# K's bias added by VectorE, ScalarE's bias rows, and value rows spread by identity columns

## The reference

```python
mod = (_silu(c) @ wmod).reshape(16, 6, 1, -1)          # sa, ca, ga, sb, cb, gb
h = _layernorm(x) * (1 + ca) + sa
# attention on h
Q = elu(h @ Wq + bq) + 1;  K = elu(h @ Wk + bk) + 1;  V = h @ Wv + bv
KV = einsum('nshd,nshm->nhmd', K, V);  Ksum = K.sum(axis=1)
Z = 1 / (einsum('nlhd,nhd->nlh', Q, Ksum) + 1e-6)
y = einsum('nlhd,nhmd,nlh->nlhm', Q, KV, Z) @ Wo + bo
x1 = layer_norm(h + y) * g1 + beta1
z = layer_norm(x1 + relu(x1 @ W1 + b1) @ W2 + b2) * g2 + beta2
x = x + ga * z
h2 = _layernorm(x) * (1 + cb) + sb
# channel mix on h2, with h2 shifted by one token as x_prev
out = x + gb * sigmoid(xr @ W_r.T) * (square(relu(xk @ W_k.T)) @ W_v.T)
```

## Time and profile before

| | |
|---|---|
| median of three runs | 163.07 us (162.75 to 163.19) |
| the profiled execution | 162.81 us, span 160.7 us |
| busy: PE, PEld | 155.6 us (97%), 145.1 us (90%) |
| busy: DVE, ACT, POOL | 123.1, 127.3, 104.6 us |
| granted PE clock | 1.00 over the span |
| DMA | 9.94 MB, mean 62 GB/s |

### The profile page before, as it was taken

The page is one execution under the profiler, slowest core; times in us unless marked ns, Lnnn a source line. Parts: engine busy times, 40 slices in busy tenths (PEclk is TensorE's granted clock), DMA queues, the critical chain, the costliest instruction groups (busy, mean ns, idle before and its releaser), DMA issues.

```text
span 160.7 us, 4111 instructions
## 1 busy us (share of the span) xinstructions
PE 155.6 (97%) x1151; PEld 145.1 (90%) x1151; DVE 123.1 (77%) x572; ACT 127.3 (79%) x346; POOL 104.6 (65%) x243
## 2 busy tenths in 40 slices
PE   7899999999999999999999999999999999999992
PEld 6778998999999999999999999999999999888891
DVE  3766878597887969696978779796969777888842
ACT  4256777889797979898997979797989989656562
POOL 4337567576676767787676767676877755973631
PEclk9999999999999999999999999999999999999999
DMA  4926299920010101010100101010101001010112
GB/s 122 269 90 174 67 276 369 423 115 0 2 37 0 33 0 33 4 37 0 34 5 0 33 4 35 0 35 4 33 0 35 4 0 33 2 37 0 35 33 67
DMA packets 8974, 9.94 MB, mean 62 GB/s; under 512 B 724, under 2 KB 7416, under 8 KB 8952
## 3 DMA queue, kind: packets, MB, share of 16 engines
q1 hardware_dynamic: 8656, 9.60, 18.8%
q10 hardware_dynamic: 296, 0.08, 0.2%
HBM read 7.55 MB, written 2.13 MB: 60 GB/s over the span
## 4 chain that ended last, share of the span: by engine, by line
PE 93%; DMA 2%; DVE 2%; ACT 1%; issue 0%; SPq 0%; DVEq 0%
PE bank L1266 16%; PE bank L1156 16%; PE bank L1145 8%; PE bank L1238 5%; PE bank L1194 5%; PE bank L1150 5%; PE bank L1222 4%; PE bank L1182 4%; PE bank L1230 4%; PE bank L1378 4%; PE bank L1210 4%; PE bank L1206 4%; PE bank L1249 3%; DMA kqvo<-in_kqvo 2%; PE bank L1219 1%; PE bank L1398 1%
## 5 line engine op out<-in xcount | busy, mean ns | idle before, releaser
L1156 PE MATMUL bank<-w,hid 128*128 128x128 f32 x240 | 31.7, 275 | 0.0
L1266 PE MATMUL bank<-x1T,w 128*128 128x256 f32 x120 | 30.9, 381 | 0.0
L1156 PEld LDWEIGHTS bank<-w,hid 128*128 128x128 f32 x240 | 29.3, 192 | 0.0
L347 ACT ACTIVATE hid<-bank,b_cols 128x256 f32<-128x256 f32 x60 | 26.0, 511 | 1.1 <-PE bank L1266 1.1
L544 POOL TENSOR_TENSOR rstd_n<-vare_n,power 128x2 f32<-128x2 f32 x30 | 23.8, 792 | 2.4
L1266 PEld LDWEIGHTS bank<-x1T,w 128*128 128x128 f32 x120 | 21.5, 190 | 2.7 <-DVE z L803 0.2
L710 DVE TENSOR_SCALAR ny<-bank,mv_ny,rstd_ny 128x128 f32<-128x128 f32 x32 | 11.7, 406 | 9.0 <-POOL rstd_ny L544 9.0
L323 ACT ACTIVATE hT<-bank,modT 128x256 f32<-128x256 f32 x16 | 9.0, 565 | 11.3 <-PE bank L1145 11.3
L540 POOL TENSOR_TENSOR vare_n<-mv_n,eps 128x2 f32<-128x2 f32 x30 | 5.9, 195 | 17.2 <-DVE mv_n L704 17.1
L292 ACT ACTIVATE n<-x_all,shift_n,rstd_n 128x128 f32<-128x128 f32 x27 | 11.8, 485 | 2.5 <-POOL shift_n L552 2.5
L317 ACT ACTIVATE keepT<-bank,modT 128x255 f32<-128x255 f32 x26 | 13.1, 555 | 0.0
(11 more groups left out here) (187 smaller groups left out, 454.7 us busy)
## 6 DMA issues: line engine op xcount, KB each, us to landing
gm_rows<-mod_rows_dram SPq DMA_DIRECT2D x2, 960.0 KB, 9.5
out<-out_sb SPq DMA_DIRECT2D x15, 128.0 KB, 1.8
gm_rows<-mod_rows_dram SPq DMA_DIRECT2D x1, 768.0 KB, 6.7
w<-in_w SPq DMA_DIRECT2D x1, 512.0 KB, 5.6
x_all<-in_x SPq DMA_DIRECT2D x1, 512.0 KB, 5.6
bv_row<-bv_rows_dram SPq DMA_DIRECT2D x1, 512.0 KB, 7.1
bv_row<-bv_rows_dram SPq DMA_DIRECT2D x1, 384.0 KB, 4.4
gm_rows<-mod_rows_dram SPq DMA_DIRECT2D x1, 384.0 KB, 3.7
```

Of the source, the lines that this page charges most:

```text
L347: last = nc.scalar.activation(hid[:, f, :], bank[:, f % 2 * L:(f % 2 + 1) * L], ACT.Relu, bias=b1_cols[:, f:f + 1])
L1156: last = nc.tensor.matmul(banks[6][:, c * D:(c + 1) * D], hid[:, f, c * 128:(c + 1) * 128], w2[:, f, :], start=False, stop=(f == FF - 1 an ...
L1266: return nc.tensor.matmul(bank[:, f % 2 * L:(f % 2 + 1) * L], w1[:, f * 128:(f + 1) * 128], x1T[:, :], start=True, stop=True)
```

## The change

1. **K's bias.** For items 1 to 15 `k_product` no longer starts with the bias matmul. DVE adds the bias: `k_biased(s)` reads bank 4 and `bias_rows` and writes `kb` in SBUF. `k_exponent` and `k_elu` read `kb` from then on, and the bank is free for the next writer once `kb` is made. For item 0 the bias goes in through a f32 matmul of the identity with `bias_rows`.
2. **The bias rows.** `bias_rows` is made in the opening by PE (Wk's product with `bo`, minus `bk` through one row of -1) and one ACT operation; the bf16 split on DVE and its tiles go.
3. **The opening.** The first transposes take an `n1` made as `(x - mean) * rstd` by DVE (`normalise`), which needs no shift; the first `hT` gets a shift column of its own (`shift_first`). ACT makes both halves of the `n1` that the state product needs. Three warm-up matmuls go.
4. **Value rows.** `bv_product` is one matmul, early; DVE adds `bv` (`bv_rows`), and `direct_row(s)` is one matmul of an identity column, broadcast, with `bv_rows`.
5. **The step on DVE.** `centred` comes first, then `denominators`, `reciprocals`, `k_biased`, `attention`; the K half of the mix moves ahead of `k_elu`; the statistics of x are taken two items ahead, at the end of the step. POOL's `first_scale` moves behind `norm_scale("ny")`; `rstd` and `shift` of `n1` have two buffers.

```diff
+            act.wait_ge(bias_mm, 1)
+            act.wait_ge(const_pool, 1)
+            nc.scalar.activation(bias_rows[:, :], banks[6][:, D:2 * D], ACT.Identity, scale=-1.0,
+                                 bias=one_pair[:, 0:1]).then_inc(bias_rows_ok, 1)
...
             def k_exponent(s):
-                need(act, k_mm, s + 1)
-                nc.scalar.activation(exp_k[:, :, :], chunked(banks[4]), ACT.Exp, bias=neg1[:, :]).then_inc(expk_ok, 1)
+                if s == 0:
+                    act.wait_ge(k_mm, 1)
+                need(act, kb_ok, s)
+                source = kb[:, :, :] if s else chunked(banks[4])
+                nc.scalar.activation(exp_k[:, :, :], source, ACT.Exp, bias=neg1[:, :]).then_inc(expk_ok, 1)
...
-                h_turned(0)
+                act.wait_ge(hT_mm, 1)
+                nc.scalar.activation(hT[0][:, :], banks[0][:, 0:L], ACT.Identity, scale=mod_col(CA, 0),
+                                     bias=shift_first[:, :]).then_inc(hT_ok, 1)
+                n1_part(0, 1).then_inc(n1_ok, 1)
...
+                if live(t + 2):
+                    first_scale(sa + 2)
...
+            normalise("n1", n1[1], x_chunk(0), 1, n1_turn)
             dve.wait_ge(cols_mm, 1)
             nc.vector.tensor_scalar(modT[:, CA, :], banks[1][:, 0:S], 1.0, None, ALU.add).then_inc(cols_ok, 1)
+            nc.vector.tensor_tensor(shift_first[:, :], banks[1][:, 128:129], cols[:, BO:BO + 1], ALU.add).then_inc(cols_ok, 1)
...
             def k_elu(s):
                 need(dve, expk_ok, s + 1)
-                nc.vector.scalar_tensor_tensor(k_sb[:, :, :], exp_k[:, :, :], 1.0, chunked(banks[4]), ALU.min,
-                                               ALU.max).then_inc(k_ok, 1)
+                plain = kb[:, :, :] if s else chunked(banks[4])
+                nc.vector.scalar_tensor_tensor(k_sb[:, :, :], exp_k[:, :, :], 1.0, plain, ALU.min, ALU.max).then_inc(k_ok, 1)
+
+            def k_biased(s):
+                need(dve, k_mm, s + 1)
+                need(dve, bias_rows_ok, 1)
+                nc.vector.tensor_tensor(kb[:, :, :], chunked(banks[4]), bias_rows[:, :].unsqueeze(1).broadcast_to([128, NC, D]),
+                                        ALU.add).then_inc(kb_ok, 1)
...
                 x_stats(1)
                 x_mv(1)
+                dve.wait_ge(bv_loaded, 16)
+                dve.wait_ge(bv_mm, 1)
+                nc.vector.scalar_tensor_tensor(bv_rows[:, :], bv_bias[:, :], 1.0 / 128, banks[6][0:S, 2 * D:3 * D], ALU.mult,
+                                               ALU.add).then_inc(bv_ok, 1)
                 k_elu(0)
                 direct_weights(0)
-                q_elu(0)
+                dve.wait_ge(hT_mm, 1)
                 n1_chunk(1, 0)
                 n1_chunk(1, 1).then_inc(n1_ok, 1)
+                q_elu(0)
                 dve.wait_ge(const_pool, 9)
...
                 reciprocals(0)
+                k_biased(1)
                 attention(0)
+                direct_weights(1)
                 k_elu(1)
...
                 attention(1)
+                k_biased(2)
                 y_norm(0)
...
+                if live(t):
+                    centred(sp_)
+                    denominators(sb_)
+                    reciprocals(sb_)
+                    k_biased(sa)
+                    attention(sb_)
+                    if live(t - 4):
+                        mix_half(K_W, sc)
+                    k_elu(sa)
+                    middle(sp_)
+                    need(dve, x2_ok, sp_ + 1)
+                    norm_stats("n3", lambda c: x2_p[:, c, :])
+                    if live(t - 4):
+                        mix_half(R_W, sc)
+                    norm_mv("n3", sp_ + 1)
+                    y_stats(sb_)
+                    q_elu(sa)
+                    norm_mv("ny", sb_ + 1)
+                    if live(t + 2):
+                        x_stats(t + 2)
+                        x_mv(t + 2)
+                    masked_state(sa)
+                    shift_of_n3(sp_)
+                    y_norm(sb_)
+                    return
+
...
             def bv_product():
 
-                nc.tensor.matmul(banks[6][0:S, 2 * D:3 * D], modT[:, ROW, :], wv, start=True, stop=False)
-                nc.tensor.matmul(banks[6][0:S, 2 * D:3 * D], part128[:, 0:S], bv_pad[:, :], start=False, stop=True).then_inc(bv_mm, 1)
+                pe.wait_ge(cols_ok, 4)
+                pe.wait_ge(wvo_loaded, 16)
+                nc.tensor.matmul(banks[6][0:S, 2 * D:3 * D], modT[:, ROW, :], wv, start=True, stop=True).then_inc(bv_mm, 1)
 
             def direct_row(s):
 
-                pe.wait_ge(cols_ok, 3)
-                pe.wait_ge(wvo_loaded, 16)
-                pe.wait_ge(bv_loaded, 16)
-                dest = banks[2][:, s * D:(s + 1) * D]
-                nc.tensor.matmul(dest, modT[:, ROW, s:s + 1].broadcast_to([128, 128]), wv, start=True, stop=False)
-                nc.tensor.matmul(dest, part128[:, :], bv_pad[:, :], start=False, stop=True).then_inc(direct_mm, 1)
+                pe.wait_ge(bv_ok, 1)
+                nc.tensor.matmul(banks[2][:, s * D:(s + 1) * D], ident[0:S, s:s + 1].broadcast_to([S, 128]), bv_rows[:, :],
+                                 start=True, stop=True).then_inc(direct_mm, 1)
 
...
             def k_product(s):
 
+                if s == 0:
+                    pe.wait_ge(bias_rows_ok, 1)
+                    nc.tensor.matmul(chunked(banks[4]), ident[:, :], bias_rows[:, :].unsqueeze(1).broadcast_to([128, NC, D]),
+                                     start=True, stop=False)
+                    bv_product()
+                elif s == 1:
+                    pe.wait_ge(k_ok, 1)
                 need(pe, hT_ok, s + 1)
-                need(pe, k_ok, s)
+                need(pe, kb_ok, s - 1)
                 need(pe, tanh_ok, s - 4)
-                nc.tensor.matmul(chunked(banks[4]), ones3[:, :], bias_parts[:, :].unsqueeze(1).broadcast_to([128, NC, D]),
-                                 start=True, stop=False)
                 for c in range(NC):
                     last = nc.tensor.matmul(banks[4][:, c * D:(c + 1) * D], hT[s % 2][:, c * 128:(c + 1) * 128],
-                                            wk, start=False, stop=(c == NC - 1))
+                                            wk, start=(s > 0 and c == 0), stop=(c == NC - 1))
                 last.then_inc(k_mm, 1)
...
+                pe.wait_ge(n1_turn, 1)
+                transpose_in(banks[0], n1[1], hT_mm)
                 k_product(0)
                 q_product(0)
-                bv_product()
+                direct_row(0)
                 state_product(0)
+                value_of_state(0)
+                n1_transposes(1)
+                second_modulation((2, 5), 2)
+                attention_product(0)
+
+                k_product(1)
+                q_product(1)
                 pe.wait_ge(direct_ok, 1)
                 direct_row(1)
-                value_of_state(0)
-                second_modulation((2, 5), 2)
-                n1_transposes(1)
```

More of the change, by code:

```diff
@@ L290, in take_n1 @@
                 wait_x(act, s)
-                for c in chunks:
-                    last = nc.scalar.activation(n1[s % 2][:, c, :], x_all[:, NC * s + c, :], ACT.Identity,
-                                                scale=rstd["n1"][:, c:c + 1], bias=shift_n1[:, c:c + 1])
+                for c in range(NC):
+                    last = n1_part(s, c)
                 last.then_inc(n1_ok, 1)
-            take_n1(0, (0,))
+            act.wait_ge(bias_mm, 1)
+            act.wait_ge(const_pool, 1)
+            nc.scalar.activation(bias_rows[:, :], banks[6][:, D:2 * D], ACT.Identity, scale=-1.0,
+                                 bias=one_pair[:, 0:1]).then_inc(bias_rows_ok, 1)
+            act.wait_ge(x_in[0], 16)
+            act.wait_ge(shift_n1_ok, 1)
+            n1_part(0, 0)
             act.wait_ge(cols_ok, 2)
@@ L367, in first_steps @@
                 state_out(0)
-                act.wait_ge(bv_mm, 1)
-                nc.scalar.activation(bv_rows[:, :], banks[6][0:S, 2 * D:3 * D], ACT.Copy).then_inc(bv_ok, 1)
+                act.wait_ge(cols_ok, 5)
+                h_turned(1)
                 raw_columns(0)
-                h_turned(1)
                 k_exponent(1)
@@ L708, in normalise @@
                 need(dve, rstd_ok[name], count)
+                scale = rstd_n1[0] if name == "n1" else rstd[name]
                 for c in range(NC):
-                    last = nc.vector.tensor_scalar(dest[:, c, :], source(c), mv[name][:, c, 0:1], rstd[name][:, c:c + 1],
+                    last = nc.vector.tensor_scalar(dest[:, c, :], source(c), mv[name][:, c, 0:1], scale[:, c:c + 1],
                                                    ALU.subtract, ALU.mult)
@@ L977, in step @@
-                if live(t):
-                    q_elu(sa)
-                if not y_first:
-                    norm_mv("ny", sb_ + 1)
-                if t == S:
-                    y_norm(sb_)
-                    gated(sc)
```

(9 more changed lines are left out.)

161 lines of the change are left out of this document (59 added, 102 removed).

## The result

The changed kernel takes 163.58 us (median of 10 runs, 163.48 to 163.94), the kernel before in the same session 162.94 (10 runs, 162.37 to 163.26). The ratio is 1.0044, 95% interval 1.0031 to 1.0058: slower, by 0.6 to 0.7 us. The profiled execution took 163.68, with a span of 161.9 against 160.7.

A forecast was written before the change was run, and what follows sets the result against it. It took the ScalarE chain from the ny transposes to the attT copy as pacing, with PE also at its limit. 0.77 + 0.20 + 0.12 - 0.06 = +1.03 us gave 163.84 or 164.1, taken as 164.0; range 163.2 to 165.3.

The forecast's parts named there:

- Part 1: K's bias matmul leaving PE for 15 of 16 items: 0.107 us each, 1.6 on PE alone, taken as 0 for steps 3 to 15.
- The rival that PE alone paces: Every removed PE slot counts, 15 x 0.107 = 1.6 us, giving 161.4; chance 0.13.
- the one that the source is free: K's sum is in time and reading SBUF costs nothing: steps stay at 8.78, some 162.8; chance 0.22.
- Part 2: K's sum on DVE in front of exp_k: +0.07 us a step, 0 to 0.15; 0.77 for steps 5 to 15.
- The source: exp_k on ACT reading kb from SBUF instead of the bank: +0.05 us a step, bounds 0 and 0.10.
- the lateness: exp_k waiting for DVE's sum in a steady step: 0.02 us late, from on time to 0.06 late.
- The rival of a sum 0.2 late: DVE's sum clearly late, passing one to one into attT and the step: 166.3 us at 0.2 late; chance 0.13.
- The idle time of 0.1 to 0.2 in front of the output product: Expected sign in the changed profile: idle time on PE's loads in front of the output product, released by attT.
- Step 4 at +0.20: Step 4 costs more because step 3's y_norm still holds VectorE, so z's statistics start some 0.26 later: +0.20 us.
- Step 3 at +0.12: Without keeps on ACT, exp_k waits for the sum, starting about 26.90 instead of 26.35: +0.12 us, 0.05 to 0.2.
- Opening at -0.06: Opening up to the first hidden product: of 0.6 us gained, 0.06 remains; bounds -0.5 and +0.15.

The follow-up runs named there:

- e1: Kernel before without K's bias product for batch items 1 to 15 (bias left out for them): 0.9991 of the kernel before.
- e11: Changed kernel without DVE's K bias sum for items 3 to 15 (bias left out), exp_k and k_elu reading the bank: 162.57 us, 0.9980 of the kernel before.
- e2: Kernel before with the attT copy put ahead of the first hidden activation on ScalarE: 1.0011 of the kernel before.
- e4: Changed kernel with the attT copy put ahead of the first hidden activation on ScalarE: 162.09 us, 0.9953 of the kernel before.
- e6: Changed kernel with K's bias sum written back into the bank, exp_k and k_elu reading it there: 1.0054 of the kernel before.
- e3: Kernel before without K's bias product for items 1 to 15 and with attT copied ahead of the first hidden activation: 0.9992 of the kernel before.
- e7: Changed kernel with K's bias sum behind centred, ahead of denominators and reciprocals on VectorE, in every step: 1.0028 of the kernel before.
- e12: As e9, with value rows of items 0 and 1 spread by a product over 128 partitions instead of 16: 161.69 us, 0.9910 of the kernel before.
- e9: Changed kernel, attT copy ahead of the first hidden activation in steps 4 to 15, K's sum ahead of denominators in step 3 alone: 161.73 us, 0.9919 of before.

## Why the prediction was right, and where it wasn't

Forecast 164.0 with 0.55 for slower; measured 163.58. From the medians of before that is +0.93 forecast and +0.64 measured.

- **Part 1 at nothing.** Right, for the reason given: e1 and e11 show the nothing, e2 and e4 that attT's place held it there. The rival that PE alone paces fell, and so did the one that the source is free (e6). What the prediction didn't see is that the same product also covered hT, so that behind an early attT it is worth 0.03 a step on the kernel before (8.74 in e3 against 8.77 in e2) and 0.06 in the changed order (8.71 in e4), not 0.107.
- **Part 2 at 0.07 a step.** Measured 0.06 (8.84 against 8.78 before, and against 8.78 in e11). The source is 0.04 to 0.05, the lateness 0.04 instead of 0.02, less 0.03 that attT got shorter (0.39 instead of 0.42, for which no run gives a reason). All three were seen in rows. The rival of a sum 0.2 late fell. The idle time of 0.1 to 0.2 in front of the output product, which was to show it, isn't printed in steady steps.
- **Step 4 at +0.20.** Steps 4 and 5 together cost 0.17, in another split: 0.03 and 0.14. e7, with its steps of 8.85, has 8.83 and 8.85 there: with step 3 mended, step 5 is no longer special.
- **Step 3 at +0.12.** A mis-sized term: it cost 0.24. The sum ended at 27.27 and exp_k started at 27.31, where 26.90 was expected. Of this 0.26 is the opening; counted from hT, exp_k came after 2.09 where 1.94 was expected (26.90 - 24.96), and attT after 3.57 instead of 3.42. The error is in when DVE comes to the sum, behind z's statistics, centred, den and the reciprocal. Some 0.1 of it can be read off: z's statistics start 0.17 ahead of hT instead of 0.28 and no longer wait for PE, because x's statistics, moved to the end of the step before "at no cost", now stand in front of them. e7 shows the place of the sum: with the sum ahead of den the step is 7.68 against 7.65 before.
- **Opening at -0.06.** The largest miss, and wrong by its sign: +0.26 in this profile. The gain was smaller than forecast and was gone earlier: 0.70 instead of about 1.0 at the second K product, 0.13 instead of 0.6 at the third, 0.03 instead of 0.49 at the second attention on DVE. The loss behind it, item 2's sum and exp_k's wait for it, was sized right: from that attention to attT 1.63 us (17.54 to 19.17), where 1.59 was expected (17.08 to 18.67) and 1.02 was before. Of the 0.46 that is missing at the attention, about 0.16 is the pace of the first microseconds (below), and 0.11 the second value row over 16 partitions: its 0.28 had been priced at nothing, and 0.11 is what e12 still has of them there. The other 0.2 is open. In e9, with the same opening at a faster pace, step 3 starts 0.10 later than before, not 0.06 earlier.

The terms came to +1.03, and the spans differ by 1.2 in the profiles and 1.0 in the medians. That the sum fits is in part luck: the opening and step 3 cost 0.44 more than their terms, steps 4 to 15 0.20 less (0.77 instead of 0.97). And the forecast put the same 2.1 us around the span of both kernels, where the changed one has 1.75; without that it would have been nearer the measured 163.58, but no term of it foresaw this. The stated range is wider than its own reason: 0.01 and 0.13 a step alone give 163.3 to 164.7.

## What to carry to other kernels

Look at how far each weight load leads its matmul. In these traces the same load leads by 0.11 where its operand is early and by 0.05 or less where it is late; that wait shows in no idle time and hardly in busy shares, and the tile that the load waits for names the chain that paces. Take work from an engine only after asking what the removed instruction was covering; here it covered one wait (attT) outright and half of another (hT). Where two limits lie this close, neither edit alone gives anything: e1 nothing, e2 nothing, and one line moved behind another in the changed kernel, with its lighter TensorE, 1.5 us (e4). The short first steps need a look of their own, since they want another order (e9).

## What the runs showed of the hardware

- A product whose weights have 16 partitions stood alone: its load starts with its matmul (both at 12.76), 0.33 behind the end of the load before, and the next load starts with its own matmul too (13.17), so the slot is 0.41 long. With 128 partitions the loads lead by 0.22 and 0.11 (12.74 for 12.96, 13.07 for 13.18), and the slot is 0.22 (e12).
- In the same place of the step, VectorE's sum of 128x256 took 0.36 us to SBUF and 0.41 to the bank that it read (e6). In other places the sum to SBUF took 0.41 and 0.42 as well (17.95 in the opening, 69.54 in e7), so the place counts as much as the target.
- In the first microseconds TensorE's rows show a half pace that ends at another time in each profile, with the same opening too. By windows, the changed kernel and then e4, which has the same opening (columns of the earlier trace rows):

```profile
3.86:5.30 1.44, 1.44 (x7) 1.44 (x7) 0.74 (x7) 0.00 (x0) 0.94 (x3) 1.00 0.88 209
```

```profile
3.86:5.30 1.44, 1.44 (x11) 1.44 (x10) 0.74 (x7) 0.15 (x1) 0.91 (x2) 1.00 0.81 194
```

The granted clock is given as 1.00 in both, that is 2.4 GHz, behind warm-up products that keep the engine busy from 1.10 on. Yet the first has 7 matmuls in the stretch and the second 11, and the modulation products take 0.21 a piece in the changed kernel (from 5.30) and 0.11 in e4 (from 4.95). That is half the pace, as 1.2 GHz would give it; whether it is the clock no row shows. What stands behind moves with it, by up to 0.35 us: step 3's hT is at 25.00 in e4, 25.22 in the changed kernel and 25.35 in e11, whose openings are the same. So openings are to be compared between profiles of the same pace. The changed kernel's profile is an ordinary one for it, with a span of 161.9 against a median of 161.85.
